# Expert loads in batches of thirteen, y's two sums side by side, planes spread over later steps, maxima unscaled on ScalarE

## The reference, cut to what matters

```python
x = x + 0.5 * ffn(layernorm(x))            # 4096 rows of 128
x = x + attn(layernorm(x), context)        # 8 heads of 128, 512 keys
x = x + 0.5 * ffn(layernorm(x))            # the same weights again

def ffn(x):                                # one expert of 8 for each row
    top_idx = argmax(x @ gate_w.T + gate_b + expert_bias)
    out = sum over e of (top_idx == e) * (relu(x @ w1[e] + b1[e]) @ w2[e] + b2[e])
def attn(x, context):
    sim = (q @ k.T) * SCALE; mean = sim.mean(-1)
    attn = softmax((sim - mean) * 1.5 + mean)
    return concat_heads(attn @ v) @ Wout + bout
```

## Time and profile before

| | us |
|---|---|
| median of 3 runs (749.84 to 751.33) | 750.04 |
| profiled execution, its own time | 749.31 |
| span of that execution's trace | 747.5 |
| PE busy | 680.0 (91%) |
| DVE busy | 623.6 (83%) |
| ACT busy | 514.6 (69%) |
| POOL busy | 342.0 (46%) |

### The profile page before, as it was taken

The page is one execution under the profiler, slowest core; times in us unless marked ns, Lnnn a source line. Parts: engine busy times, 40 slices in busy tenths (PEclk is TensorE's granted clock), DMA queues, the critical chain, the costliest instruction groups (busy, mean ns, idle before and its releaser), DMA issues.

```text
span 747.5 us, 16976 instructions
## 1 busy us (share of the span) xinstructions
PE 680.0 (91%) x5175; PEld 454.4 (61%) x5175; DVE 623.6 (83%) x1854; ACT 514.6 (69%) x1151; POOL 342.0 (46%) x437
## 2 busy tenths in 40 slices
PE   8785988889999999999999999999999998998882
PEld 7664877755555655655656655565565555777771
DVE  7688776889899899899899989989989998586662
ACT  4676666667778767867867777876786876555550
POOL 7054566524334346335435544634633543364443
PEclk9898899999999999999999999999999999999997
DMA  9910143220000000000000000000000010032110
GB/s 250 316 34 10 48 97 89 58 63 11 1 1 2 1 1 16 1 0 12 5 1 8 8 1 2 15 2 1 15 2 1 12 48 0 17 95 63 53 47 5
DMA packets 31029, 26.41 MB, mean 35 GB/s; under 512 B 5001, under 2 KB 26159, under 8 KB 30944
## 3 DMA queue, kind: packets, MB, share of 16 engines
q1 hardware_dynamic: 26496, 18.67, 8.8%
q0 software_dynamic: 3520, 6.40, 3.2%
q10 hardware_dynamic: 928, 0.27, 0.2%
HBM read 15.78 MB, written 10.47 MB: 35 GB/s over the span
## 4 chain that ended last, share of the span: by engine, by line
PE 55%; DVE 31%; issue 5%; SPq 3%; POOL 2%; ACT 1%; DMA 1%; POOLq 0%; DVEq 0%; ACTq 0%
PE bank L1602 11%; PE bank L1604 10%; PE bank L1603 10%; DVE neg_max L1484 9%; DVE probsT_lo L1493 9%; PE bank L1860 8%; PE bank L1652 5%; DVE neg_max_unscaled L1487 3%; PE bank L1677 2%; PE bank L1653 2%; SPq L448 1%; PE bank L1662 1%; DVE hT_lo L1332 1%; POOL rows L642 1%; PE bank L1903 1%
## 5 line engine op out<-in xcount | busy, mean ns | idle before, releaser
L658 POOL TENSOR_SCALAR probs<-probs,row_inv 128x512 f32<-128x512 f32 x256 | 177.1, 692 | 270.1 <-DVE row_inv L1498 268.8
L891 ACT ACTIVATE probs<-bank,neg_max_unscaled,unscale_bits 128x512 f32<-128x512 f32 x256 | 199.0, 777 | 117.2 <-DVE neg_max_unscaled L1487 115.4
L1484 DVE TENSOR_REDUCE neg_max<-bank 128x1 f32<-128x512 f32 x256 | 176.0, 687 | 22.6 <-PE bank L1604 17.1
L1493 DVE TENSOR_TENSOR probsT_lo<-bank,probsT_hi 128x512 f16<-128x512 f32 x256 | 174.5, 682 | 3.8 <-ACT probsT_hi L898 3.7
L1860 PEld LDWEIGHTS bank<-ident,probs 128*128 128x128 f32 x1024 | 126.1, 142 | 64.9 <-issue 18.7
L1860 PE MATMUL bank<-ident,probs 128*128 128x128 f32 x1024 | 155.5, 275 | 8.0 <-DVE probsT_lo L1493 8.0
L898 ACT ACTIVATE probsT_hi<-bank 128x512 f16<-128x512 f32 x256 | 150.3, 587 | 3.3 <-PE bank L1860 3.3
L1602 PE MATMUL bank<-probsT_hi,vw_hi 128*128 128x512 f16 x256 | 98.1, 383 | 7.8 <-DVE probsT_lo L1493 6.7
L1602 PE MATMUL bank<-m_hi,xT_hi 128*128 128x512 f16 x256 | 97.0, 379 | 0.5 <-ACT probs L891 0.4
L1603 PE MATMUL bank<-probsT_lo,vw_hi 128*128 128x512 f16 x256 | 97.3, 380 | 0.0
L1604 PE MATMUL bank<-probsT_hi,vw_lo 128*128 128x512 f16 x256 | 97.3, 380 | 0.0
(11 more groups left out here) (261 smaller groups left out, 1167.5 us busy)
## 6 DMA issues: line engine op xcount, KB each, us to landing
w_raw<-in_L_ffn_w SPq DMA_DIRECT2D x16, 256.0 KB, 5.1
x_packed<-slot_rows SPq DMA_DIRECT2D x39, 65.5 KB
slot_rows<-slots SPq DMA_DIRECT2D x39, 65.5 KB, 1.8
x_stats<-rows SPq DMA_DIRECT2D x4, 524.0 KB, 9.4
rows<-x_packed SPq DMA_DIRECT2D x8, 262.0 KB, 2.7
rows<-in_L_attn_x SPq DMA_DIRECT2D x4, 512.0 KB, 8.2
slot_rows<-x_stats,row_of_slot POOLq DMA_INDIRECT x39, 2.9
out<-slot_rows POOLq DMA_INDIRECT x39, 2.5
```

The lines of the kernel that those rows point to most:

```text
L658: pool.tensor_scalar(PR[:, u % 4, :], PR[:, u % 4, :], RI[:, u % 4:u % 4 + 1], 2.0 ** P_BITS, ALU.mult, ALU.mult).then_inc(normed, 1)
L891: act.activation(PR[:, n % 4, :], score_bank(n)[:, :], ACT.Exp, bias=NMS[:, n % 4:n % 4 + 1], scale=MUN, accum_out=SU[:, n % 4:n % 4 + 1]) ...
L1484: v.tensor_reduce(NM[:, n % 4:n % 4 + 1], score_bank(n)[:, :], AX.X, ALU.max, negate=True)\
L1493: v.tensor_tensor(PTL[at], BK[2 + u % 2][:, :].rearrange("p (c q) -> p c q", c=KC), PTH[at], ALU.subtract).then_inc(pT_lo, 1)
```

## The change

Five edits. (1) `BATCH` goes from 4 to 13: the batches are 0-12, 13-16, 17-29 and 30-38, four loads to an FFN for eleven. (2) In the FFN's step DVE does the two additions of y one after the other, ahead of `hT_lo`. (3) In the first FFN the planes are spread out again: the bias planes are made before the FFN, `ww_square` and w2's high planes a step or more later, w2's low planes of experts 0 to 2 on POOL and of 3 to 7 on DVE in steps 5 to 9 (before: 0 to 4 on DVE in steps 2 to 6, 5 to 7 on POOL), `scales` in step 8 for step 4, and attention's planes start in step 9 for step 5. (4) In attention `neg_max` is multiplied by MUN on ACT, just ahead of the exp that uses it, and no more on DVE. (5) `probsT` has three buffers instead of two, and the product with vw comes nine units after the scores instead of eight.

```diff
-    BATCH = 4
+    BATCH = 13
...
-        LAG_T, LAG_AV = 3, 8
+        LAG_T, LAG_AV = 3, 9
...
-        SCALES_AT, NORMS = 4, 3 * P
+        SCALES_AT, NORMS = 8, 3 * P
...
-        SPLIT_STEP = 5
+        SPLIT_STEP, BIAS_AT = 9, 4
...
-        W2_HIGHS = {1: [2, 3], 2: [4], 3: [5], 4: [6], 5: [7]}
-        W2_LOWS = {2: [0], 3: [1], 4: [2], 5: [3], 6: [4]}
-        POOL_LOWS = range(5, E)
+        W2_HIGHS = {1: [2], 3: [3], 4: [4], 5: [5], 6: [6], 7: [7]}
+        W2_LOWS = {5: [3], 6: [4], 7: [5], 8: [6], 9: [7]}
+        POOL_LOWS = range(0, 3)
...
+                if h == BIAS_AT:
+                    bias_high(1)
+                if h == BEFORE_FFN - 1:
+                    bias_high(2)
...
-                    if r == 0 and m in (1, 2):
-                        ww_square(m - 1)
+                    if r == 0 and m in (2, 3):
+                        ww_square(m - 2)
...
             def slot(n):
                 if unit(n):
+                    act.wait_ge(neg_max, n + 1)
+                    act.activation(NMS[:, n % 4:n % 4 + 1], NM[:, n % 4:n % 4 + 1], ACT.Copy, scale=MUN)\
+                        .then_inc(neg_max_ready, 1)
                     act.wait_ge(neg_max_ready, n + 1)
...
-                    if u % G == 0 and u // G >= 2:
-                        act.wait_ge(av, G * (u // G) - G)
+                    if u % G == 0 and u // G >= 3:
+                        act.wait_ge(av, G * (u // G) - 2 * G)
...
+                        dve.wait_ge(s_yhi, SLOTS * r + j + 1)
+                        v.scalar_tensor_tensor(out=row, in0=BK[6 + j % 2][:, D:2 * D], scalar=YUN, in1=row,
+                                               op0=ALU.mult, op1=ALU.add).then_inc(s_fin, 1)
...
-                    dve.wait_ge(neg_max, n + 1)
-                    v.tensor_scalar(NMS[:, n % 4:n % 4 + 1], NM[:, n % 4:n % 4 + 1], MUN, None, ALU.mult)\
-                        .then_inc(neg_max_ready, 1)
```

More of the change, by code:

```diff
@@ L181, in macaron_kernel @@
         with ExitStack() as ffn:
-            ATT_PLACE = sb("room_2", [P, 7168], fp32, ffn)
+            ATT_PLACE = sb("room_2", [P, 9216], fp32, ffn)
             HTH = sb("hT_hi", [P, 3, FC * P], fp16, ffn)
@@ L188, in macaron_kernel @@
             PR = sb("probs", [P, 4, KEYS], fp32, att)
-            PTH = sb("probsT_hi", [P, 2, KC, G * P], fp16, att)
-            PTL = sb("probsT_lo", [P, 2, KC, G * P], fp16, att)
+            PTH = sb("probsT_hi", [P, 3, KC, G * P], fp16, att)
+            PTL = sb("probsT_lo", [P, 3, KC, G * P], fp16, att)
         XN = XNB[:, 0, :].rearrange("p (g d) -> p g d", g=G)
@@ L613, in w2_low @@
             def w2_low(e):
-                done = 2 * (e - POOL_LOWS[0])
+                done = 2 * e
                 pool.wait_ge(w2_hi, e + 1)
@@ L628, in _ @@
                 gather(j + LEAD)
-                if j == R - LEAD - 1:
-                    for e in POOL_LOWS:
-                        w2_low(e)
+                if j in POOL_LOWS:
+                    w2_low(j)
                 for h, part in split_at(j + 5, 1):
@@ L668, in _ @@
             rounds(slot)
-            for i in range(1, G):
+            for i in range((LAG_AV - 5) // 2, G):
                 sort_tile(NG - 2, i)
@@ L895, in slot @@
                     act.wait_ge(pT_ps, u + 1)
-                    if u % G == 0 and u // G >= 2:
-                        act.wait_ge(av, G * (u // G) - G)
-                    act.activation(PTH[:, (u // G) % 2, :, (u % G) * P:(u % G + 1) * P],
+                    if u % G == 0 and u // G >= 3:
+                        act.wait_ge(av, G * (u // G) - 2 * G)
+                    act.activation(PTH[:, (u // G) % 3, :, (u % G) * P:(u % G + 1) * P],
                                    BK[2 + u % 2][:, :].rearrange("p (c q) -> p c q", c=KC), ACT.Copy)\
@@ L905, in slot @@
                     ln_keep(g, turn_bank(g))
-                for g in after(n, 8, 1):
+                for g in after(n, 9, 1):
                     o_evac(g)
@@ L1333, in step @@
                                                in1=HTH[:, j % 3, :], op0=ALU.max, op1=ALU.subtract).then_inc(s_hlo, 1)
[L1334 to L1338, removed]
-                                               op0=ALU.mult, op1=ALU.add).then_inc(s_fin, 1)
                     if live(m, 0):
@@ L1491, in slot @@
                     dve.wait_ge(pT_hi, u + 1)
-                    at = (slice(None), (u // G) % 2, slice(None), slice((u % G) * P, (u % G + 1) * P))
+                    at = (slice(None), (u // G) % 3, slice(None), slice((u % G) * P, (u % G + 1) * P))
                     v.tensor_tensor(PTL[at], BK[2 + u % 2][:, :].rearrange("p (c q) -> p c q", c=KC),
@@ L1640, in step @@
                             pe.wait_ge(bias_scaled, 2)
-                        if r == 0 and j < E:
-                            pe.wait_ge(w2_lo, min(j + 1, POOL_LOWS[0]))
                         if r == 0 and j in POOL_LOWS:
-                            pe.wait_ge(w2_lo_pool, 2 * (j + 1 - POOL_LOWS[0]))
+                            pe.wait_ge(w2_lo_pool, 2 * (j + 1))
+                        elif r == 0 and j < E:
+                            pe.wait_ge(w2_lo, j + 1 - len(POOL_LOWS))
                         pe.wait_ge(s_hlo, SLOTS * r + j + 1)
@@ L1682, in step @@
                         head_rest(BEFORE_FFN + m)
-                    if r == 0 and m == 3:
+                    if r == 0 and m == SCALES_AT - 1:
                         pe.wait_ge(ctxT_squares, WW_SQUARED)
@@ L1851, in slot @@
                             pe.wait_ge(o_kept, g - 1)
-                    three(BK[4 + g % 2][:, :], VWH[:, h, c, :], VWL[:, h, c, :], PTH[:, hh % 2, c, :],
-                          PTL[:, hh % 2, c, :], h == 0 and c == 0, h == H - 1 and c == KC - 1).then_inc(av, 1)
+                    three(BK[4 + g % 2][:, :], VWH[:, h, c, :], VWL[:, h, c, :], PTH[:, hh % 3, c, :],
+                          PTL[:, hh % 3, c, :], h == 0 and c == 0, h == H - 1 and c == KC - 1).then_inc(av, 1)
                 if unit(n - LAG_T):
```

3 lines of the change are left out of this document (removed).

## The result

| | before | changed |
|---|---|---|
| median, us (runs) | 750.68 (4) | 728.66 (4, 726.75 to 731.46) |
| ratio, 95% interval | | 0.9705, 0.9666 to 0.9745 |
| profiled execution, us | 749.31 | 726.75 |
| span, us | 747.5 | 725.0 |
| PE, DVE, ACT busy, us | 680.0, 623.6, 514.6 | 675.6, 592.5, 578.7 |

What follows compares the result with a forecast made beforehand. Attention was taken as bound by PE's pace plus DVE's backlog. Terms -16.5, -5.5, +0.5, -1.2 and +3 summed to -19.7 us against the profiled 749.31, forecasting 729.5 us, range 716 to 739.

Steps and rivals of the forecast that it cites:

- Edit 4's prices: Attention: the product on ACT takes 0.30 us, ACT's slot becomes 1.54, DVE's 1.27, the loop of both 1.57.
- Attention, -16.5: Attention with its tail: edits 4 and 5 save 16.5 us, 14.5 of PE's waits and 2 in the tail; bounds -22 and -8.
- the tail's -2: From the last scores to the second FFN's second step: 2 us less of 13.4.
- 1.0 of waiting: Attention: PE's waiting in a full group of 32 slots falls from 3.1 us to 1.0.
- The 22 us of waiting: Attention: PE waits 22 us over the eight groups before the change, of which 7.5 remain.
- Edit 3, -5.5: First FFN: moving planes and `scales` brings PE to step 10 at 79.0 for 85.41, saving 5.5 us; bounds -8 and -2.
- Attention's planes, +0.5: Before attention's first scores: its planes end four steps later, costing 0.5 us; bounds 0 and +2.
- Edit 2, -1.2: FFN: `slot_done` comes 0.6 us earlier, `hT_lo` 0.4 later, saving 1.2 us with the last scatters; bounds -2.5 and 0.
- Edit 1, +3: Both FFNs: longer loads of expert numbers and low clock behind a 3 us stop cost 3 us; bounds -8 and +9.
- fixed price: FFN loads of expert numbers cost the same whatever their size: -8 in place of +3, 718.3 us; chance 0.17.
- ScalarE bounds the slot: Attention: ScalarE paces every slot if product and exp's wait reach 0.55 us; at 0.78, 800 us; chance 0.03.

Runs made afterwards that it cites:

- u_planes: The changed kernel with edit 3 undone (planes, scales and square sums in their earlier steps): 766.19 us, 0.976 of the kernel before.
- u_rows: The changed kernel with edit 2 undone (second addition of y behind `hT_lo` again): ratio 0.9684 to the kernel before.
- before_again: The kernel before, unchanged, profiled on the later runs' slower chip: 791.85 us.
- control: The changed kernel itself, run again on another chip: 755.33 us, 0.9543 of the kernel before.
- b_four: The changed kernel with BATCH = 4 again, so edit 1 alone undone: 751.56 us, 0.9488 of the kernel before.
- x_twice: The changed kernel with ScalarE's one-column product done twice in each slot, once into a spare buffer: 765.69 us, 0.9717 of the kernel before.
- b_shift: The changed kernel with BATCH = 4 and the table of expert numbers 12 bytes later in memory: 745.81 us, 0.9426 of the kernel before.

## Why the prediction was right, and where its sum was not

The mechanisms of edits 4 and 5 held, and the time lay well inside the range. That 729.5 came so close to the median of 728.66 is partly luck. Against the profiled execution, from which the sum started, it was 2.8 us too high (726.75), and three terms were off by 2 to 4 us, not all the same way: attention gave less than forecast, edit 3 more, and edit 1 cost nothing where I had put 3.

- **Edit 4's prices** held: product 0.293 (0.30), ACT's slot 1.57 (1.54, and 1.57 for the loop), ACT 45.9 us busy in 50 (46). DVE's slot of 1.3 is nowhere to be seen alone: in the free slots it follows ACT's 1.57.
- **Attention, -16.5 forecast, -14.3 measured** (-12.4 and -1.9; the tail's -2 was right). The full group fell by 1.5 us and not by 2.1: I left 1.0 of waiting and 1.5 is there, since 59.2 - 55.36 - 2.3 = 1.5. Group by group the gain is 1.6, 0.7, five times 1.5 to 1.6, and 2.3 us. The 22 us of waiting that I started from was too much: the waits that the trace itself has for PE between the first and the last scores are 13.3 us before and 6.6 now.
- **The split** between the two edits I hadn't made: the runs give 5.5 us to edit 4 and 6.6 to edit 5. The later product takes away a wait that a faster VectorE doesn't.
- **Edit 3, -5.5 forecast, about -9 measured** (step 10 9.3 us earlier on the first chip; `u_planes` puts 10.5 to 12.0 of it on edit 3). The sum had a slip: 85.41 - 79.0 less 0.5 is 5.9. The step that failed is "it now stands in step 8, with the same cost and the same wait behind it". `scales` costs 1.50 us there for 2.73, and w2's low plane ahead of it 0.74 for 1.63. PE waited 1.63 us and not 3, and the clock stayed at 1.00 behind it, so the 1.5 us of low clock that I added didn't come.
- **Attention's planes, +0.5:** the step from tile 38 to the first scores grew by 0.9, of which 0.6 is a wait for `vw_lo`.
- **Edit 2, -1.2:** not seen in `u_rows`. On the other chips the second FFN, whose steps only edits 1 and 2 change, takes from tile 0 to tile 37 97.8 us with neither edit (`before_again`), 92.9 without edit 2, 91.4 without edit 1 and 92.7 with both: there each seems to cover for the other, by one trace of each.
- **Edit 1, +3 forecast, about 0 measured.** The sizes of the stops were as forecast, 3.28 us for 3.06 and 2.25 for 2.2. What I had added to them was too much: 1.0 in each FFN for the first load of thirteen, which doesn't show as idle time, and 1.6 of low clock. The low clock came behind the shorter stop and cost about half of that: the three steps from y of tile 27 on take 130.90 - 124.00 = 6.9 us for 3 x 2.02. On the first chip the stretch behind step 10 of the first FFN stayed as it was (63.4 and 63.3 us) and the second FFN grew by 0.3. The clock's fall that I cited from the earlier trace rows stood behind waits of 0.71 and 1.44 us, not behind a stop of 3; one of 3.05 had a low clock behind it too (0.54 at 62 to 64 us), but the two of 3.3 here did not. In the second FFN the two stops that are no longer there ahead of tile 12 bought nothing, as PE then waited 2.57 us for tile 12's rows, with low clock behind it. The control against `b_four` gives 1.2 us in the second FFN and 3.8 in all, with an interval too wide to tell it from 0 or 6. The rival "fixed price" is refuted.
- **Rival "ScalarE bounds the slot":** its point, 0.55 (0.57 by its own numbers), was near, but too high. `x_twice` puts x at 0.32 + 0.19 = 0.51 us, and attention is already 5 us slower than before.

The Trainium skill, "Runtime: NRT & Kernel Launch", "Instruction fetch mechanics", has about 200 ns for each register. The traces' 3.28 us for thirteen (0.25 each) and 1.1 for four off the boundary (0.27 each) agree roughly; 0.4 for four on it does not. The Trainium skill, "DMA: Bandwidth & Descriptors", "Latency and other measured facts", has a floor of about 600 ns to a load. By it fourteen loads fewer should have saved 8.4 us (an estimate), and no run shows such a gain; the aligned four at 0.4 us lies under that floor.

## What to carry to other kernels

When a producer is late, both a faster producer and a later consumer pay, and they may add up: undo each alone before crediting one. Before moving work from a full engine to an emptier one, compare its slot (not its busy share) with the bound's: here ScalarE went from 1.23 to 1.57 us under a bound of 1.73, and another 0.19 would have lost everything. A small instruction's price read in a crowded step is not its price elsewhere (`scales` took 2.73 us there and 1.50 here), and where a table lies in memory can be worth more than how it is batched.

## What the runs showed of the hardware that was not expected

**A 128x2 operation of DVE took as long as GpSimd's instruction beside it.** In the kernel before, DVE's timeline and then GpSimd's:

```profile
68.85 1.63 DVE L1218 SCALAR_TENSOR_TENSOR w_hi_lo<-w_raw,w_then_w_scale_bits,w_hi_lo 128x512 f16<-128x512 f32 x1
...
71.30 1.09 DVE L1235 SCALAR_TENSOR_TENSOR bound_quarters<-bound_exponents_f 128x2 f32<-128x2 f32 x1
```

```profile
71.22 1.15 POOL L621 TENSOR_TENSOR w_hi_lo<-w_raw,w_hi_lo 128x512 f16<-128x512 f32 x1 [0.18 <-POOL w_raw L617]
```

DVE's instruction ends at 72.39 and GpSimd's at 72.37. The same one takes 0.16 us in the changed kernel, where GpSimd has done its planes by then, and 1.09 again in `u_planes`. The other traces show the same. In all fourteen together, DVE began an instruction of 128x512 that makes a low plane (`w_lo`, `w_hi_lo`) thirty times while GpSimd worked on a plane: each of these ended 0.53 to 0.56 us after GpSimd's. The 263 instructions of this kind (`m_lo` too) that began with no such work beside them took 0.74 to 0.80 us. Six tiny ones (`bound_exponents`, `bound_quarters`) ended within 0.03 us of GpSimd's. `hT_lo`, one of whose inputs lies in PSUM, took its usual 0.68 beside one (at 66.45 us in the kernel before). `scales` and the plane ahead of it are 2.1 us of the 2.9 by which PE came to step 10 earlier than forecast: edit 3 moved GpSimd's planes away from them. The Trainium skill, "GPSIMD Engine Reference", "Specifications", says that GpSimd shares its SBUF interfaces with VectorE and contends with instructions that have two SBUF inputs or run in a 2-port mode. The rows agree for those with two inputs; `bound_exponents` has one, and no row shows its mode. No run moved GpSimd's planes alone.

**A register load of four numbers costs 0.4 us on a multiple of 16 bytes and 1.1 elsewhere**, shown by `b_shift`. Loads of thirteen and nine numbers off it took 3.3 and 2.3 us. What an aligned load of more than four costs is not seen: the one of tiles 0 to 12 lies behind queued matmuls.

**Two one-column products in a row cost 0.29 + 0.19 us**, as the second starts 0.19 behind the first when nothing waits between them.

**The clock fell behind a stop of 2.25 us and not behind one of 3.28**, so a stop's length alone doesn't tell. In the control's second FFN it is the other way round, at the same two loads: 0.50 behind 3.16 us and 1.00 behind 2.30 (the control, columns as above):

```profile
688.00:690.00 2.00, 2.00 (x18) 1.77 (x16) 0.45 (x2) 0.66 (x2) 0.00 (x0) 0.50 0.11 35
...
718.00:720.00 2.00, 2.00 (x31) 1.74 (x29) 1.61 (x6) 1.27 (x4) 0.41 (x1) 1.00 0.15 32
```

**Stops of ACT of up to 7.4 us with no known releaser** come in the two FFNs of the other three chips. One, of 5.2 to 7.4 us, stands at the same place in all twelve traces from there: ahead of `slot_xT_hi` of tile 9 in the second FFN.
